# Two state-space layers as one program of 64 chunks, with each image's norm formed inside the loop

## The reference, cut to what matters

```
seq = x.transpose(0, 2, 1, 3).reshape(b * n, t, f)          # 256 sequences of 128 steps, 64 features
u, z = split(seq @ W_in.T)                                  # 128 inner channels each
u = silu(causal_conv4(u) + conv_b)
dt = softplus((u @ W_x.T)[:R] @ W_dt.T + b_dt);  Bmat, Cmat = 16 states each
h_t = exp(dt_t * A) * h_(t-1) + (dt_t * u_t) * B_t;  y_t = sum over the 16 states of h_t * C_t
out = ((y + u * Dp) * silu(z)) @ W_out.T
```

## Time and profile before

| | us |
|---|---|
| median of 3 runs (lowest, highest) | 6244.23 (6240.84, 6248.35) |
| the profiled execution | 6251.4 |
| its span, first to last instruction | 6249.6 |
| TensorE, weight loads, VectorE, ScalarE, GpSimd busy | 5093, 2638, 4940, 3286, 4765 |
| layer 0: its own block from, first u, last add | 73.7, 86.7, 1934.0 |
| layer 1: first u, last u, last add | 2004.0, 3744.3, 3850.2 |

### The profile page before, as it was taken

How to read it: one execution, slowest core, us unless ns; L and a number is a source line. 1 busy time by engine, 2 the same in 40 slices (tenths; PEclk the granted TensorE clock), 3 DMA queues, 4 the chain that set the end, 5 groups by cost and what they waited for, 6 DMA issues and landing times. The chain is left out here.

```text
span 6249.6 us, 78158 instructions
## 1 busy us (share of the span) xinstructions
PE 5093.4 (81%) x22462; PEld 2637.8 (42%) x22462; DVE 4940.1 (79%) x6854; ACT 3285.8 (53%) x3643; POOL 4764.7 (76%) x2174
## 2 busy tenths in 40 slices
PE   3888888888884888888888887881548989989897
PEld 1333333333332343333433344520225656656565
DVE  5999999999995999999999997105457676776665
ACT  3555555555552555555555553000436767767776
POOL 3999999999993999999999996000236767767675
PEclk9999999999996999999999998795779999999999
DMA  3555555555552555555555553491348999999999
GB/s 129 202 197 199 205 201 197 201 203 205 199 197 81 196 205 197 201 201 206 200 201 199 205 199 126 171 402 32 79 102 161 188 168 188 181 172 188 186 188 207
DMA packets 1423977, 1150.93 MB, mean 184 GB/s; under 512 B 1216728, under 2 KB 1226096, under 8 KB 1415792
## 3 DMA queue, kind: packets, MB, share of 16 engines
q1 hardware_dynamic: 1423858, 1149.56, 64.9%
HBM read 814.23 MB, written 21.09 MB: 134 GB/s over the span
## 5 line engine op out<-in xcount | busy, mean ns | idle before, releaser
L633 POOL TENSOR_TENSOR l_state<-l_state,l_c_row 128x1024 f32<-128x1024 f32 x1024 | 2405.0, 2367 | 73.9 <-DVE l_state L593 69.4
L469 PE MATMUL l_y_ps<-l_state,ident 128*128 128x512 f32 x4096 | 1992.3, 613 | 47.4 <-POOL l_state L633 46.8
L1495 POOL TENSOR_TENSOR l3s_el<-l3s_s_sb,l3s_eh 128x1024 f16<-128x1024 f32 (+2 forms) x584 | 1168.7, 2012 | 1129.0 <-ACT l3s_s_sb L1480 1117.0
L593 DVE TENSOR_TENSOR_SCAN l_state<-l_decay,l_b_ps 128x1024 f32<-128x1024 f32 x704 | 1608.9, 2285 | 73.4
L469 PEld LDWEIGHTS l_y_ps<-l_state,ident 128*128 128x128 f32 x4096 | 784.8, 196 | 869.8 <-issue 679.6
L1503 DVE TENSOR_SCALAR_CACHE_REDUCE l3s_s_sb<-l3s_s_ps 128x512 f32<-128x512 f32 (+1 forms) x1096 | 753.2, 689 | 490.2 <-PE l3s_s_ps L1439 468.2
L1452 PE MATMUL l3s_o_ps<-l3s_vt,l3s_et 128*128 128x257 f16 x4368 | 878.5, 279 | 204.6 <-DMA l3s_et<-l3s_el 143.6
L1479 ACT ACTIVATE l3s_eh<-l3s_s_sb,l3s_shift 128x1024 f16<-128x1024 f32 (+2 forms) x584 | 634.6, 1087 | 548.0 <-DMA l3s_et<-l3s_el 448.3
L579 DVE TENSOR_TENSOR l_b_ps<-l_dtu,l_b_ps 128x1024 f32<-128x1024 f32 x704 | 850.4, 1208 | 31.2 <-PE l_b_ps L457 29.4
L457 PE MATMUL l_b_ps<-l_bc,mamba_pick 128*128 128x512 f32 x1408 | 575.6, 491 | 292.0 <-DVE l_state L593 282.4
L1454 PE MATMUL l3s_o_ps<-l3s_vt,l3s_et 128*128 128x129 f16 x4368 | 787.9, 224 | 0.0
(11 more groups left out here) (356 smaller groups left out, 5439.9 us busy)
## 6 DMA issues: line engine op xcount, KB each, us to landing
l_c_row<-l_c_rows SPq DMA_DIRECT2D x1024, 512.0 KB, 3.8
l_b_row<-l_c_rows SPq DMA_DIRECT2D x320, 512.0 KB, 5.0
l_ring_a<-in_L_conv_W SPq DMA_DIRECT2D x28, 1024.0 KB, 10.9
l2b_ring_b<-in_L_conv_W SPq DMA_DIRECT2D x26, 1024.0 KB, 10.9
l_xs<-X SPq DMA_DIRECT2D x64, 256.0 KB, 5.4
l_ring_a<-in_L_conv_W SPq DMA_DIRECT2D x14, 704.0 KB, 12.7
l2b_ring_b<-in_L_conv_W SPq DMA_DIRECT2D x13, 704.0 KB, 12.7
l_ring_a<-in_L_conv_W SPq DMA_DIRECT2D x14, 640.0 KB, 12.1
```

The source lines that it names most:

```text
L469: last = nc.tensor.matmul(y_ps[:, half(h)], C["ident"][:, :], state[:, s % STATES, half(h)], start=False, stop=(s == S - 1))
L593: nc.vector.tensor_tensor_scan(state[:, s % STATES, :], by, add, 0.0, ALU.mult, ALU.add).then_inc(s_scan, 1)
L633: nc.gpsimd.tensor_tensor(state[:, s % STATES, :], state[:, s % STATES, :], c_row[:, s % C_ROWS, :], ALU.mult).then_inc(s_hc, 1)
L1495: nc.gpsimd.tensor_tensor(el[:, part, off:off + EXPW], s_sb[:, par, j * EXPW:(j + 1) * EXPW], eh[:, part, off:off + EXPW], ALU.subtract).t ...
```

## The change

The constants, both layers' weights and the norm of image 0 of layer 0 are now formed in one block, `prepare`. X is loaded by SP with a semaphore for each image, the 18 weight loads go out from ScalarE. One block, `mamba_layers`, then runs 64 chunks, all written out for every engine; chunk c takes its weights from layer c // 32 and its columns from c % 32. The norms are ten jobs j: 0 to 3 are the images before layer 0, 4 to 7 those before layer 1, 8 and 9 images 0 and 1 before layer 2. Job 0 is done in `prepare`; the statistics of job 1 stand ahead of u in the prep of chunk 0; those of jobs 2 to 9 stand behind the scan of unit 15 in chunks 0, 4, 8, 16, 24, 32, 40 and 48, 32 instructions in one go. The rest of a job is spread over four later chunks (its phases): small VectorE instructions at units 1, 3, 5 (phases 0 and 1) and 8, 9, 11, 12, 14 (phase 2), copies of a row at units 1 and 3 (phase 3), sums over the partitions on TensorE at unit 14, their reads by VectorE at unit 15, and the root as a logarithm and an exponential on ScalarE at units 5 and 6 of phase 2. The mean matrix is now a matrix of ones, with the factors in the instructions that read the sums. c_out is no longer a tile of its own but gu; its write moves to unit 8 and ahead of the load of xs, and the overwrite of gu at unit 9 waits for it. The statistics of `top_blocks` begin at image 2.

More of the change, by code:

```diff
@@ L98, in vector @@
             for e in range(4):
-                for b in range(B):
-                    nc.vector.bn_stats(out=stats[:, bass.ds(g * 24 + (e + b * G) * 6, 6)],
+                for b in range(self.first, B):
+                    nc.vector.bn_stats(out=stats[:, bass.ds(g * 24 + (e + (b - self.first) * G) * 6, 6)],
                                        in_=Xv[:, b, :, bass.ds(g * 8 + e * 2, 2)]).then_inc(self.s_stats, 1)
-        dve.wait_ge(self.s_stats, B * G)
+        dve.wait_ge(self.s_stats, self.cols)
         steps = [0]
@@ L369, in mamba_layer, with weights, columns @@
         s_out = sem(f"{tag}_out_product")
-        s_x = sem(f"{tag}_x_updated")
+        s_add = sem(f"{tag}_x_updated")
+        def weights(c):
+            return Ms[c // CHUNKS]
+        def columns(c):
+            c %= CHUNKS
+            return slice(c * COLS, (c + 1) * COLS)
         def half(h):
@@ L434, in pe_prep @@
                 for h in range(2):
-                    last = nc.tensor.matmul(prep_ps[:, half(h)], M["w_bc"][:, :], u[:, half(h)], start=True, stop=True)
+                    last = nc.tensor.matmul(prep_ps[:, half(h)], weights(n)["w_bc"][:, :], u[:, half(h)], start=True, stop=True)
                 last.then_inc(s_pbc, 1)
@@ L440, in pe_prep @@
                 for h in range(2):
-                    last = nc.tensor.matmul(prep_ps[:, half(h)], M["w_dt"][:, :], u[:, half(h)], start=True, stop=True)
+                    last = nc.tensor.matmul(prep_ps[:, half(h)], weights(n)["w_dt"][:, :], u[:, half(h)], start=True, stop=True)
                 last.then_inc(s_pdt, 1)
@@ L477, in pe_out @@
             else:
-                wait(pe, s_x, c)
+                wait(pe, s_add, c)
             for n in range(CHUNK_N):
@@ L636, in is_first, with norm_reads_before @@
         def is_first(c):
-            return isinstance(c, int) and c == 0
+            return c == 0
+        def norm_reads_before(c):
+            return sum(1 for k in SUM_OF if k < c) + 3
+        def pe_norm(pe, c):
[25 more added lines that the diff above has]
+                norm.read(dve, spare_ps, *SUM_OF[c])
         def behind(c, par, s, lag):
```

405 lines of the change are left out of this document (218 added, 187 removed).

## The result

| | median us (lowest to highest) | profiled span |
|---|---|---|
| before | 6243.19 (6232.59 to 6254.21), 6 runs | 6249.6 |
| after | 6267.03 (6259.90 to 6272.24), 6 runs | 6270.4 |

The ratio is 1.0037, 95% interval 1.0025 to 1.0050. The kernel became 0.4% slower; 6166 us and a clear gain had been forecast.

The account below looks back on a forecast made before the run. VectorE was taken to set the loop's pace, with GpSimd following about 1 us a chunk to spare. 34.5 + 99.4 - 48 - 8 = 78 us off 6244 gave 6166 us, own range 6148 to 6203, widened to 6132 to 6212.

Parts of the forecast that it names:

- The small steps (added): VectorE in the loop: most small norm instructions hide in drive-to-scan holes; 8 us lost, bounds 5 and 24.
- The bursts: Behind unit 15's scan in eight chunks, 32 statistics cost VectorE 6.0 us each time: 48 us lost, bounds 43 and 58.
- bursts are free: Rival, loop: GpSimd is the true bound, so VectorE's pauses eat only slack; 48 us less, 6118; chance 0.05.
- bursts cost double: Rival, loop: pauses empty GpSimd's and TensorE's queues, which restart late; 12 us a burst, 6214; chance 0.08.
- The seam: Between the layers: drain, semaphore clearing, weight loads, statistics, chain, columns and first prep all go; 99.4 us saved, bounds 98 to 101.
- The start: Opening block: weights load beside X and only image 0 is needed; block starts at 39.2, 34.5 us saved, 25.5 to 43.5.
- t0: Opening block: time at which the second layer's weights have landed; taken as 20 us, bounded by 11.2 and 29.0.
- what stands behind it, 19.15: Opening block after the weights land: taps, 32 statistics, turned copies, chained steps, reads, copies and column products, 19.15 us in sum.
- Nothing: the rest: Moved c write, later xs load, statistics after the layers, semaphores and written-out chunks: no time gained or lost.
- written-out streams stall: Rival, loop: issue of 64 chunks of new code falls behind and VectorE waits; at 2 us a chunk 6294; chance 0.05.
- unrolling gains: Loop written out: without taken branches instruction fetch gains a little, at most 0.8 us a chunk; the trace does not bear it out.
- the halved sums: Block after the layers: statistics take 12.4 us less, but VectorE's 17.64 us wait for TensorE grows, so nothing is gained.

Follow-up runs that it names:

- the probes changed places: Eight kinds of small VectorE instruction, rotating over eight units from chunk to chunk, added to the changed kernel stripped of the loop's small norm work: 6379.54 us, one run.
- the run of bursts only: The changed kernel without the loop's steps, row copies, sums, reads and roots, every chunk normalised with image 0's values of layer 0: 6163.97 us, ratio 0.9864.
- both kernels with probes: Eight small VectorE instructions a chunk added to the changed kernel without the loop's small norm work: each kind at one unit, 6464.74 us; kinds rotating, 6379.54 us.

## Why the prediction was wrong, point by point

**The step that failed is "The small steps (added)": 8 us, with 24 as its upper bound.** Measured alone they lengthen the loop by 101.6 us. I priced them at 0.11 us, the pitch of small copies in the block before the loop, where GpSimd is idle, and let nearly all vanish in the hole of 0.23 us between drive and scan. The hole is there, and bn_stats do fit it. But in the loop GpSimd is busy 98% of the time, and an instruction of 0.19 us that stands still until a 2.36 us one has ended takes longer by what is left of it: 0.38 to 1.65 us on the mean in eleven of the thirteen step instructions of the changed kernel (only L219 and L234 stay at 0.20 and 0.21), and 1.05 to 1.40 where the probes changed places. No row of before shows such an instruction beside a busy GpSimd, and the upper bound, all 24 instructions of a job exposed, never asked whether their price held there. Had I taken as a bound that each step instruction stands still for half a GpSimd instruction, 1.18 us, 9 jobs of 13 are 138 us (an estimate, to be set against the measured 101.6), and 34.5 + 99.4 - 48 - 138 gives a kernel that is 52 us slower. The Trainium skill's rule on the port pair, cited above, speaks against this part of the change by itself, and I did not weigh it.

**The bursts (48 us)** were right: 50.1 in the loop. The rivals *bursts are free* (6118) and *bursts cost double* (6214) fell with the run of bursts only at 6163.97.

**The seam (99.4 us)** was right: two u lie 56.4 us apart across the change of layer, and the loop of before is 101.6 us longer than 62 mean intervals of layer 1. Layer 0's own mean is 56.81 instead of 56.73, which makes up the 2.2 beyond the forecast.

**The start (34.5 us)** was too large by its term t0, taken as 20 and measured as 27.24, within its bounds; what stands behind it, 19.15, measured 18.1. The first xs load came 28.4 us earlier. At the second u only 24.8 are left, since 41.3 us instead of 38.7 lie between the first two u: small steps of image 1 stand there. The Trainium skill's rule of turns between queues (page "DMA: Bandwidth & Descriptors") did come true in this trace: 428 packets of each queue from 6.2 to 21 us. What did not come true is the conclusion that I drew from it, a t0 near 11: with turns by packet, each small packet of the weights waits for a 16 KB one of the images, 0.55 us on the mean, and 2528 of them on 16 DMA engines are not through before the images are. Beside this one issue was held for 12.96 us. That the images are the cause is shown by the kernel that holds the last three back; by what means they hold the issue, no run shows.

**Nothing: the rest.** The written-out streams cost nothing and gained nothing. So the rival *written-out streams stall* is wrong, although it was the one on the right side of zero; and the Trainium skill's page "Runtime: NRT & Kernel Launch", by which unrolling gains, has nothing to show here either. In the block after the layers VectorE's wait for TensorE grew from 17.64 us to 29.72, as forecast, and ate the halved sums. A new wait of 5.0 us in 1600 stands at L756, for ScalarE's copy of B and C. The 10.3 us by which the part behind the last u was shorter lie in the last stretch, from GpSimd's first L1721 (L1495 in the kernel before) to the end: 1881.5 us before, 1871.3 after, and 1872.3 to 1878.0 in the ten other kernels, all with the same work there. Their cause stays open, and one execution before is not enough to say that they are more than scatter.

In sum: 24.8 + 101.6 - 157.5 + 10.3 = -20.8 us, where 34.5 + 99.4 - 48 - 8 = 78 was forecast. The shortfall of 99 us is the steps (94), what steps and bursts cost together beyond their sum (6), the start (10) and the bursts (2), less the seam (2) and the tail (10).

## What to carry to other kernels

Before a small instruction is put on VectorE beside a busy GpSimd, look at its operands: with one input in PSUM, or as bn_stats, tensor_reduce or memset, it costs 0.2 us or less (a bn_stats of 128x128 0.28); as an SBUF-to-SBUF copy, a tensor-by-scalar or with two SBUF inputs it costs what is left of GpSimd's running instruction, here 0.4 to 1.65 us on the mean, by where it falls. Such work was better put on GpSimd itself (0.2 to 0.3 us each, although that was the busier engine: 12.8 us of loop instead of 101.6), or done by another instruction. And a duration read in a stage where the other engine idles is no price for one in which it runs; the standing still is found in the mean length of instructions, never in the waits. And small loads beside large ones are to be counted in packets: in turns by packet, many small ones are the slow side.

## What was not expected of the hardware

- A 128x32 f32 instruction of VectorE took 1285 (copy), 1397 (tensor by scalar) and 1050 ns (two SBUF inputs) beside GpSimd's instructions of 2.36 us, 186 to 192 ns in forms that differ only in where one operand lies or in the instruction's name, and 85 as a memset.
- GpSimd's instructions did not lengthen: the mean of its product was 2367 ns before the change, 2364 after, and 2362 in both kernels with probes. What GpSimd lost is waiting for VectorE's scan, 110.4 us instead of 27.4 in the same stretch.
- On ScalarE's queue the eleventh of 18 small weight loads stood at its issue for 12.96 us while 8 MB of images moved from SP's queue, and for 0.92 us with 2 MB of them. From 6.2 to 21 us the two queues moved 428 packets each, 6.23 MB of images and 0.07 MB of weights.
